# Edge phases of a graph layer on one core: twice the steps picked by matmul, and 51 steps fetched row by row from ScalarE's queue

## The reference, cut

```python
h0 = maximum(layernorm(x), 0)
wsum = segment_sum(edge_weight, dst)                 # per node
w = edge_weight / maximum(wsum, 1e-12)[dst]
feat = relu(h0 @ W_pool + b_pool)
neigh = segment_max(feat[src] * w[:, None], dst)     # phase 0, 0 where a node has no edge
rst = h0 @ W1_self + neigh @ W1_neigh + b1
h = relu(rst / maximum(norm(rst), 1e-12))
neigh2 = segment_sum(h[src] * w[:, None], dst) / maximum(deg, 1)[:, None]   # phase 1
out = x + relu(h @ W2_self + neigh2 @ W2_neigh + b2)
```

## Time and profile before

| | before |
|---|---|
| median of 3 executions | 4891.58 us (4890.01 to 4899.52) |
| the profiled execution's own time | 4890.01 us |
| its span, first to last instruction | 4888.3 us |
| TensorE clock granted, mean | 0.694 of full speed |
| TensorE matmuls busy | 2366.6 us (48%) |
| VectorE busy | 2557.5 us (52%) |
| ScalarE busy | 1258.6 us (26%) |
| GpSimd busy | 3055.4 us (63%) |
| moved by DMA | 500.48 MB, 102 GB/s in the mean |

### The profile page before, as it was taken

The page is one execution under the profiler, slowest core; times in us unless marked ns, Lnnn a source line. Parts: engine busy times, 40 slices in busy tenths (PEclk is TensorE's granted clock), DMA queues, the critical chain, the costliest instruction groups (busy, mean ns, idle before and its releaser), DMA issues.

```text
span 4888.3 us, 36773 instructions
## 1 busy us (share of the span) xinstructions
PE 2366.6 (48%) x8752; PEld 1102.2 (23%) x8752; DVE 2557.5 (52%) x6066; ACT 1258.6 (26%) x4008; POOL 3055.4 (63%) x3242
## 2 busy tenths in 40 slices
PE   1435555654545554545355444454545454444525
PEld 1333333222212221211231111111112111111113
DVE  1646666655555554555456544554545454545535
ACT  1523333222222222222352222222222222222220
POOL 6365555666666666666656666666666666666665
PEclk9755665666676676667677666776777676767757
DMA  4244222332322232322343332323333332333336
GB/s 137 86 132 134 89 81 95 99 100 88 98 92 89 92 97 89 97 89 91 116 114 93 103 99 93 110 91 98 106 97 107 94 109 92 108 95 109 98 108 180
DMA packets 271729, 500.48 MB, mean 102 GB/s; under 512 B 59784, under 2 KB 188552, under 8 KB 246680
## 3 DMA queue, kind: packets, MB, share of 16 engines
q1 hardware_dynamic: 167992, 286.33, 16.8%
q0 software_dynamic: 103232, 211.68, 16.4%
q10 hardware_dynamic: 288, 0.13, 0.0%
HBM read 260.07 MB, written 237.83 MB: 102 GB/s over the span
## 4 chain that ended last, share of the span: by engine, by line
another core or an unknown queue 28%; DVE 22%; issue 20%; DVEq 13%; PE 7%; ACT 6%; POOL 2%; DMA 1%; ACTq 0%; SPq 0%; POOLq 0%
DVEq L941 12%; DVE S L947 7%; DVE S L944 7%; ACT pT L696 3%; ACT pM L696 2%; POOL G L590 2%; DVE CP L963 2%; PE pH L1232 1%; PE pM L1261 1%; DVE U L1025 1%; PE pM L1197 1%; DVEq L799 1%; DVE CP L961 1%; PE pR L1261 1%
## 5 line engine op out<-in xcount | busy, mean ns | idle before, releaser
L590 POOL DMA_INDIRECT G<-feat_tab,SRC x1435 | 1360.0, 948 | 901.7 <-issue 392.9
L590 POOL DMA_INDIRECT G<-h_tab,SRC x1507 | 1421.8, 943 | 783.4 <-issue 419.8
L1261 PE MATMUL pM<-U,A 128*128 128x512 f16 x1662 | 764.4, 460 | 736.8 <-issue 419.0
L696 ACT ACTIVATE pT<-G,EW 128x128 f32<-128x128 f32 x1494 | 471.8, 357 | 1277.5 <-DVE S L944 499.4
L696 ACT ACTIVATE pM<-G,EW 128x128 f32<-128x128 f32 x1448 | 456.9, 357 | 1251.7 <-issue 533.7
L1025 DVE TENSOR_SCALAR U<-pR,kcode 128x1024 f16<-128x1024 bf16 x490 | 365.4, 746 | 392.3 <-remote 308.8
L1261 PE MATMUL pR<-U,A 128*128 128x512 f16 x980 | 448.3, 457 | 123.0 <-issue 122.1
L1232 PE MATMUL pH<-CP 128*128 128x98 bf16 x1563 | 310.6, 358 | 348.7 <-DVE CP L963 183.9
L1261 PE MATMUL pM<-CP,A 128*128 128x512 f16 x690 | 307.0, 445 | 307.9 <-issue 224.7
L1261 PEld LDWEIGHTS pM<-U,A 128*128 128x128 f16 x1662 | 181.4, 109 | 1160.6 <-issue 645.4
L947 DVE SCALAR_TENSOR_TENSOR S<-S,M,pT 128x128 f32<-128x128 f32 x782 | 271.5, 347 | 324.2 <-issue 119.7
(11 more groups left out here) (216 smaller groups left out, 2473.1 us busy)
## 6 DMA issues: line engine op xcount, KB each, us to landing
scan<-S SPq DMA_DIRECT2D x97, 1032.0 KB
scan<-S SPq DMA_DIRECT2D x97, 1024.0 KB
G<-h_tab,SRC POOLq DMA_INDIRECT x1507
G<-feat_tab,SRC POOLq DMA_INDIRECT x1435
U<-own_tab SPq DMA_DIRECT2D x48, 256.0 KB
feat_tab<-F SPq DMA_DIRECT2D x24, 256.0 KB
own_tab<-A SPq DMA_DIRECT2D x24, 256.0 KB
A<-feat_tab SPq DMA_DIRECT2D x24, 256.0 KB
```

Of the source, the lines that this page charges most:

```text
L590: pool.indirect_dma_start(out=dst, out_offset=None, in_=table, in_offset=bass.IndirectOffsetOnAxis(ap=idx, axis=0)).then_inc(s, 16)
L696: act.activation(scaled(t), v, ACT.Copy, scale=EW[:, t:t + 1]).then_inc(s_mul, 1)
L1261: ins = pe.matmul(o, AB[:, v, n, :], hot, start=(v == 0), stop=(v == NT - 1))
```

## The change

Two things are done to the source of rows; the combine, the stores, the node stages and the tables stay as they are.

**More quads.** Phase 0 gets 18 quads for 10. The first still spreads its picks over 104 steps from step 460 on, and each of the other 17 over 56 steps (before: 105). Phase 1 gets 29 quads for 14, one every 50 steps (before: 103). Each new quad brings its 49 picks, 196 matmuls, one load of row numbers, two copies, eight turning matmuls, one absolute value and one last-bit instruction.

**Rows fetched from ScalarE's queue.** 25 steps of phase 0 and 26 of phase 1 (`ROWA`) get their rows from 128 single DMAs each, issued by ScalarE: each reads one row of 512 bytes from the table at an address held in a register and writes it into one partition of one of NGS = 2 new slots (`GA`). `fetch_rows` runs at the head of `multiply` and issues RATE = 2.25 such DMAs for each step, in phase 0 for each step that isn't an early one, from the phase's start until its 3200 or 3328 rows are through. Before the first of a slot's 128 rows it waits until the step that used the slot has been multiplied; before each sixteenth it loads RL = 16 addresses from the tile `IX` into 16 registers. A fetched step is the last step of a group of four, about one block after its last row was issued (`row_step`). `multiply` of a fetched step waits for its slot's 128 rows (`s_arow`). In all there are 51 x 128 = 6528 row DMAs and 408 register loads.

The gathers are thereby 1378 in phase 0 and 1421 in phase 1: `GORD` leaves out the quads' steps and the fetched ones. A new input `srcr` (64 KB) holds the source nodes of the fetched steps; SyncE loads it into `IX` in the prologue, and DVE shifts it left by 9 to make byte addresses (`s_ix`), which ScalarE awaits before phase 0.

```diff
-Q1 = [(0, 460 + 105 * i, 105) for i in range(10)]
-Q2 = [(1, SPL + 103 * i, 103) for i in range(14)]
+Q1 = [(0, 460, 104)] + [(0, 564 + 56 * i, 56) for i in range(17)]
+Q2 = [(1, SPL + 50 * i, 50) for i in range(29)]
...
-GORD = [(0, t) for t in SEQ if (0, t) not in PAT] + [(1, t) for t in range(TS) if (1, t) not in PAT]
+RL = 16
+NGS = 2
+RATE = 2.25
+STEPS = (SEQ, range(TS))
+
+def row_step(phase, m):
+    b = (STEPS[phase][int(P * (m + 1) / RATE)] + 8 + T - 1) // T
+    return [t for t in range(T * b + 11, T * b + 7, -1) if phase or t not in XAT][0]
+
+ROWA = [(phase, row_step(phase, m)) for phase in range(2) for m in range((25, 26)[phase])]
...
+GORD = [(0, t) for t in SEQ if (0, t) not in PAT and (0, t) not in FETCHED] + \
+    [(1, t) for t in range(TS) if (1, t) not in PAT and (1, t) not in FETCHED]
...
+            def fetch_row(to, phase, reg, s):
+                at = act.snap(reg, donate=True)
+                act.dma_start(to.bitcast(U8), flat[phase][bass.ds(at, 4 * D)].rearrange("(a d) -> a d", a=1))\
+                    .then_inc(s, 16)
+
+            def fetch_rows(phase, t):
+                if t not in ORDER[phase]:
+                    return
+                n = ORDER[phase][t]
+                for q in [q for q in range(int(RATE * n), int(RATE * (n + 1))) if q < P * NRA[phase]]:
+                    k, p = phase * NRA[0] + q // P, q % P
+                    if p == 0 and k >= NGS:
+                        ph, before = ROWA[k - NGS]
+                        act.wait_ge(s_mul, ph * TS + before + 1)
+                    if p % RL == 0:
+                        ahead[:] = [act.alloc_register(f"arow{k}_{p + r}") for r in range(RL)]
+                        act.load(ahead, IX[k:k + 1, p:p + RL])
+                    fetch_row(GA[p:p + 1, k % NGS, :], phase, ahead[p % RL], s_arow[k % NGS])
+
             def multiply(phase, t):
                 n = slot_of(phase, t)
+                fetch_rows(phase, t)
                 if (phase, t) in PAT:
...
+                elif (phase, t) in AAT:
+                    k = AAT[phase, t]
+                    act.wait_ge(s_arow[k % NGS], 16 * P * (k // NGS + 1))
+                    v = GA[:, k % NGS, :]
```

More of the change, by code:

```diff
@@ L86 @@
 PAT = {(QUADS[u][0], t): (u, i) for u in range(QN) for i, t in enumerate(quad_steps(u))}
-GORD = [(0, t) for t in SEQ if (0, t) not in PAT] + [(1, t) for t in range(TS) if (1, t) not in PAT]
+RL = 16
[6 more added lines that the diff above has]
+ROWA = [(phase, row_step(phase, m)) for phase in range(2) for m in range((25, 26)[phase])]
+NRA = [len([1 for ph, t in ROWA if ph == phase]) for phase in range(2)]
+AAT = {pt: m for m, pt in enumerate(ROWA)}
+ORDER = [{t: n for n, t in enumerate(steps)} for steps in STEPS]
+assert all(t < TS and pt not in PAT for pt in ROWA for t in pt[1:])
+FETCHED = set(ROWA)
+GORD = [(0, t) for t in SEQ if (0, t) not in PAT and (0, t) not in FETCHED] + \
+    [(1, t) for t in range(TS) if (1, t) not in PAT and (1, t) not in FETCHED]
 SLOT = {pt: n for n, pt in enumerate(GORD)}
@@ L118 @@
 TWO = 0x40000000
+U8 = mybir.dt.uint8
 U32 = mybir.dt.uint32
@@ L160, in own_store_block, with build @@
     return (OWN_FIRST + OWN_EACH * (g + 1)) // T + 1
-def build(nc, x, src, srcq, dstx, ew, w_pool, b_pool, w1s, w1n, b1, w2s, w2n, b2, out):
+def build(nc, x, src, srcq, srcr, dstx, ew, w_pool, b_pool, w1s, w1n, b1, w2s, w2n, b2, out):
     feat = nc.dram_tensor("feat_tab", (NP, D), F32).ap()
@@ L184, in build @@
         G = sb("G", [P, NG, D])
+        GA = sb("GA", [P, NGS, D])
+        IX = sb("IX", [P, P], I32)
         S = sb("S", [P, NS, T, RW])
@@ L326, in build @@
         s_sst = [sem(f"s_sst{i}") for i in range(NS)]
+        s_arow = [sem(f"s_arow{i}") for i in range(NGS)]
+        s_ixl = sem("s_ixl")
+        s_ix = sem("s_ix")
         s_oh = sem("s_oh")
@@ L447, in raw_arrived @@
                 eng.wait_ge(s_x[max(i for i in range(len(LOADS)) if sum(LOADS[:i]) <= g)], 16)
+        flat = [tab.rearrange("n d -> (n d)").bitcast(U8) for tab in (feat, htab)]
         block = ctx.enter_context(nc.Block())
@@ L680, in _ @@
                     act.activation(C[:, :], M[:, :], ACT.Identity, scale=-NEG, bias=neg[:, 0:1]).then_inc(s_c, 1)
+            ahead = []
+            def fetch_row(to, phase, reg, s):
[15 more added lines that the diff above has]
+                    fetch_row(GA[p:p + 1, k % NGS, :], phase, ahead[p % RL], s_arow[k % NGS])
             def multiply(phase, t):
                 n = slot_of(phase, t)
+                fetch_rows(phase, t)
                 if (phase, t) in PAT:
@@ L721, in _ @@
             act.wait_ge(s_ew, 16)
+            act.wait_ge(s_ix, 1)
             act.wait_ge(s_h0, NGR)
@@ L1421 @@
     srcq = np.stack([srcs[:, list(quad_steps(u))].T.reshape(-1) for u in range(QN)])
-    given = [filled(x, 0, NP, 0), srcs[:, order], srcq, dstx, filled(edge_weight, 0, EP, 0),
+    srcr = filled(np.stack([srcs[:, t] for _, t in ROWA]), 0, P, 0)
+    given = [filled(x, 0, NP, 0), srcs[:, order], srcq, srcr, dstx, filled(edge_weight, 0, EP, 0),
              L0_gnn_W_pool, L0_gnn_b_pool, L0_gnn_W1_self, L0_gnn_W1_neigh, L0_gnn_b1,
```

5 lines of the change are left out of this document (4 added, 1 removed).

## The result

| | before | after |
|---|---|---|
| median | 4891.09 us (4890.01 to 4899.52, 4 runs) | 4971.02 us (4959.41 to 4978.21, 4 runs) |
| the profiled execution, its span | 4890.01, 4888.3 us | 4991.74, 4989.6 us |
| clock granted, mean | 0.694 | 0.811 |

The ratio is 1.0158, 95% interval 1.0139 to 1.0178: the change makes the kernel 1.6% slower. I had forecast 4773 us, faster by 117, and gave "slower" 0.36. The time lies inside the wide range, on the other side of no change.

What follows compares the result with a forecast made beforehand. The prediction took POOL's gathers, at 1.42 to 1.48 us each, to bound the kernel. Its terms, -99 - 63 + 45 = -117 us against 4890.0, gave 4773 us; own range 4700 to 4860, wide range 4560 to 5080.

Steps and rivals of the forecast that it cites:

- 0.31 + 0.97 = 1.28 us: ScalarE per phase 1 step: multiply plus 2.25 row DMAs at 0.43 us, hidden below the forecast pace of 1.34 us.
- The second rival: ScalarE becomes the bound: at 0.50 us a row a step takes 1.435 us, +162 us, 5052; chance 0.18.
- The pace of a gather, 1.47 and 1.50: POOL's time per gather after the change: 1.47 us in phase 1, 1.50 in phase 0 from 870 to 2340 us.
- The first rival, cover: Consumers become slower than POOL, so backlog seldom builds and every gather costs 1.41 us: 4545 us; chance 0.21.
- -99 and -63 us: Savings from removed gathers: 99 us in phase 1, 63 us in phase 0 from 870 to 2340 us.
- +45 us for the early steps: Phase 0, 404 to 870 us: loss added because ScalarE's row DMAs make 482 us of work in 466.
- The quads' waits: ScalarE's wait for TensorE's turned rows, 15.2 us each, grows with 47 quads: +143 us, 5033; chance 0.17.
- DVE's cover: DVE in phase 1: a combine and 0.98 picks need 1.10 us a step, to stay hidden; share above 0.8.
- The backlog: POOL's back-to-back gathers at 1.25 us build a backlog that ends in slow stretches; 1.41 us a gather can be held.

Runs made afterwards that it cites:

- 4.12 case: Runs in which the kernel before, run beside the experiment, took 4123 to 4130 us; the change itself took 4052.9 us beside 4123.4.
- quads_only: The change with its doubled quads but no rows fetched by ScalarE: 4006.2 us beside 4124.5 for the kernel before, ratio 0.9714.
- rows_by_sync: The change with row DMAs and register loads issued by SyncE's queue between its stores: 3950.3 us beside 4123.4 for the kernel before, ratio 0.9578.
- more_quads: No rows fetched by ScalarE, quads closer still, 54 for the change's 47: 4216.7 us beside 4124.4 for the kernel before, ratio 1.0226.
- pool_at_145: The kernel before with three chained memsets behind each gather, one gather every 1.53 us: 5040.6 us beside 4890.6 for the kernel before, ratio 1.0312.
- 4.89 case: Runs in which the kernel before took 4891 us: both profiles, the result (change 4971.02 us) and one experiment.
- change_paced: The change with three chained memsets behind each gather of the edge phases: 4701.0 us beside 4122.8 for the kernel before, ratio 1.1399.

## Why the prediction was wrong, by its steps

Between the profiled executions the time grew by 101.7 us: about 8 ahead of the first combine, -16 from there to step 500, +36 from step 500 to the end of phase 0, and +74 in phase 1 (2182 to 2256 us).

1. **"I take 0.43, the load: 0.31 + 0.97 = 1.28 us ... It is hidden, with 0.06 us to spare."** This is the step that failed. A row costs ScalarE 0.565 us in the case of the result, of which the DMA, priced at 0.43 by SyncE's loads, is only 0.342. The trace before had no row for the move (0.139) and the register load (0.084 a row), and I gave both nothing. My own bound for the failure was 0.46 us a row. By medians the three parts come to 0.42 us (0.275 + 0.061 + 1.346/16, start to start), so 0.43 was near an undisturbed row by luck: too much for the DMA, nothing for the rest. What I left out above all is that an engine with 4.4 times the instructions in its queue (8251 in the 2000 us for 1867) meets the starts at 0.70 us itself. I had given these to the other engines, as a matter of POOL's pace; they are some 0.12 us of the mean row and 0.27 us of the step. In the 4.12 case, without them, a row is 0.49 us, and ScalarE still sets a step of 1.17 us, above the 1.14 us of POOL.

   The second rival, ScalarE the bound, with 0.18, is what happened. Its step was 1.435 us and came to 1.45, but by errors that cancel: a row took 0.565 us for 0.50, and the rest of a step 0.18 us for 0.31, as the queue issues on while a multiply runs. I priced the rival at +162 us; between the medians it came to +80, and phase by phase the profiles show +74 for +55 in phase 1 and +20 for +107 in phase 0. The +107 was wrongly worked out: it sets all 1563 steps, the 88 early ones without rows too, against a stretch that ends at 2340 us, while phase 0 ran to 2378 us.

   The page "Runtime: NRT & Kernel Launch" of the Trainium skill ("Instruction fetch mechanics") gives 0.2 us a register for loads from HBM, which pointed to a dear row. The loads here, from SBUF, agree only in kind: 0.06 us a register plus some 0.35 us for each load, 0.084 us a row.
2. **The pace of a gather, 1.47 and 1.50**, was that of a POOL held by its own backlog. Measured 1.60 in both phases. The first rival, cover, is half right: TensorE's stretches at 0.70 us do vanish (73 to 4) and POOL's waits for ScalarE are shorter and more (331 in the 2000 us for 145, 480 us together for 324). But what paced POOL was ScalarE's queue at 1.45 us a step, 0.909 gathers in it, and nothing was won. This rival's own sum has a slip: 1421 x 1.41 is 2004 us and not 1990, which makes it 4559 us for 4545. So has the upper end of the range: by the second rival's sum 5080 us is a row of 0.50 us, not 0.52.
3. **-99 and -63 us** for the removed gathers became +74 and +36. That they are worth something where ScalarE is free was right in the 4.12 case: 1.28 us each in quads_only and 1.21 in rows_by_sync, for a cadence of 1.25.
4. **+45 us for the early steps** was not there: to step 500 it went 16 us faster.
5. **The quads' waits** (third rival, 0.17): the wait before the absolute value of the picked rows fell from 318.2 us to 10.7 us in 47 quads, so this rival is out. TensorE, which turns these rows, hardly had starts 0.70 us apart any more.
6. **DVE's cover** was right: 1.10 us for a combine and 0.98 picks holds, and more_quads shows the edge just behind it. DVE's share of phase 1 is 0.71, not above 0.8, because the step got longer.
7. **The backlog** (1.41 us a gather can be held) is borne out in part by pool_at_145, where the stretches go with the close cadence; the figure itself is not, since 1.53 was the only slower cadence that met this case.

What stays open: that ScalarE's queue turned the change in the 4.89 case is read from its trace (1751 of 2000 us in the queue, POOL and DVE both waiting for the multiply) and shown by taking it away only in the 4.12 case. That the late starts in that queue come from gathers in a row is a reading of the table above; change_paced was to test it. Whether the quads alone, or the rows on SyncE's queue, make the kernel faster in the 4.89 case wasn't measured: no run of them met it.

The best version measured is rows_by_sync, 4.2% faster than before and 2.5% than the change (3950.3 beside 4052.9, against the same before).

## What to carry to other kernels

A DMA issued at an address from a register brought two more instructions here: price the move and the register load with it, and charge them to what stands behind them in that engine's queue. An engine that is 29% busy can have a full queue, so sum the time between starts of its queue before adding issues to it; the same work belongs on an engine whose next instruction nobody waits for. If a trace shows stretches in which engines start an instruction late, price a queue that gets many more instructions with those late starts in it. And two savings that hold alone must be added up against the tightest engine: here 118 and 52 us made 70, and 173 once the queue was another.

## What the runs showed of the hardware

- The same kernel took 4124 us beside most experiments, and 4891 us here and beside one of them; one chip showed both. In the longer executions there are stretches, some 1450 us together, in which TensorE starts an instruction only every 0.70 us or a multiple, mostly after POOL has started 10 to 20 gathers back to back. They are gone at a cadence of 1.53 us. With 4.4 times as many instructions in ScalarE's queue the distances of 0.70 and 1.40 us appeared there, 549 in 2000 us, and left TensorE. The 75 us that the changed kernel takes longer up to its first combine have hardly any such starts.
- A gather starts every 1.25 us whether or not a memset stands behind it: 0.11 us of memset went into the 0.30 us between two gathers for +8 us in the kernel; three unchained ones made it 1.27 and three chained ones (0.43 us) 1.53.
- A row DMA on ScalarE takes 235 ns in the median and its move 29 ns; a load of 16 registers from SBUF 1.30 us, of 32 2.26 us. On SyncE's queue 36 rows with their moves and loads take 15.8 us, 0.44 us a row.
- TensorE's granted clock in phase 1 is 0.70 of full before and 0.88 after the change, with 1.9 times as many matmul instructions in the same 2000 us, and 0.95 after the change in the 4.12 case (0.75 there with the rows alone, which leave the matmuls as before).
